# A gated delta-rule scan and its routing on one core: decay inside the first product, tanh for sigmoid, a second buffer at the end

## The reference

```
a = sigmoid(h @ Wa + ba);  b = sigmoid(h @ Wb + bb)
Sk = S k_t
S  = a*S - a*b * outer(Sk, k_t) + b * outer(v_t, k_t)      # S is 8 x 8
o_t = q_t^T S
```

## Time and profile before

| what | value |
|---|---|
| timed runs | 1351.15, 1360.18, 1360.09 us; median 1360.09 |
| profiled execution | 1352.62 us, span 1350.9 us |
| TensorE busy | 989.0 us (73%) in 5924 instructions |
| VectorE busy | 846.5 us (63%) in 2008 |
| ScalarE busy | 623.9 us (46%) in 1485 |
| GpSimd busy | 442.6 us (33%) in 636 |
| chain that ended last | PE 46%, DVE 19%, issue 13%, ACT 11%, POOL 8%, DMA 2% |
| scan of the four groups | 74 to 427 us |
| barrier between the layers | 531 us |

### The profile page before, as it was taken

The page is one execution under the profiler, slowest core; times in us unless marked ns, Lnnn a source line. Parts: engine busy times, 40 slices in busy tenths (PEclk is TensorE's granted clock), DMA queues, the critical chain, the costliest instruction groups (busy, mean ns, idle before and its releaser), DMA issues.

```text
span 1350.9 us, 18007 instructions
## 1 busy us (share of the span) xinstructions
PE 989.0 (73%) x5924; PEld 600.3 (44%) x5924; DVE 846.5 (63%) x2008; ACT 623.9 (46%) x1485; POOL 442.6 (33%) x636
## 2 busy tenths in 40 slices
PE   5563074985886896888788888878788878775682
PEld 3231032443453454333334555544556545544582
DVE  1386978858988332675666566766566666624452
ACT  3435253464444253154444456643556534663272
POOL 0201352634633323022442331363241444422413
PEclk9776595996997998787888899987999988998796
DMA  7000000000000001000000323212134003331372
GB/s 221 1 0 1 0 0 1 1 1 35 1 1 1 1 0 36 1 1 1 1 1 1 114 71 105 75 36 92 33 111 122 29 18 120 106 107 46 125 218 80
DMA packets 53885, 64.67 MB, mean 48 GB/s; under 512 B 6544, under 2 KB 38304, under 8 KB 53792
## 3 DMA queue, kind: packets, MB, share of 16 engines
q1 hardware_dynamic: 51744, 59.33, 14.6%
q0 software_dynamic: 2048, 4.20, 1.0%
HBM read 52.83 MB, written 10.68 MB: 47 GB/s over the span
## 4 chain that ended last, share of the span: by engine, by line
PE 46%; DVE 19%; issue 13%; ACT 11%; POOL 8%; DMA 2%; SPq 0%; DVEq 0%; POOLq 0%; ACTq 0%
PE banks L701 8%; PE banks L844 4%; PE banks L758 4%; DVE MX L1323 3%; PE banks L554 3%; PE banks L776 3%; POOL oms L1796 3%; PE banks L748 2%; PE banks L818 2%; PE banks L711 2%; PE banks L714 2%; PE banks L606 2%; POOL QX L1695 2%; PE banks L723 2%; ACT PT L1620 1%
## 5 line engine op out<-in xcount | busy, mean ns | idle before, releaser
L1323 DVE TENSOR_REDUCE MX<-banks 128x4 f32<-128x512 f32 (+2 forms) x192 | 199.3, 1044 | 87.2 <-PE banks L818 86.5
L1774 POOL TENSOR_SCALAR_AFFINE_SELECT PT<-PT 128x256 f32<-128x256 f32 x256 | 107.0, 432 | 419.4 <-ACT PT L1620 419.1
L1620 ACT ACTIVATE PT<-banks 128x768 f32<-128x768 f32 (+1 forms) x192 | 167.9, 876 | 92.6 <-PE banks L776 91.5
L701 PE MATMUL banks<-xgT,wg 128*128 128x128 f32 x736 | 106.3, 290 | 36.1 <-ACT ysb L1581 29.5
L701 PEld LDWEIGHTS banks<-xgT,wg 128*128 128x128 f32 x736 | 92.5, 198 | 57.7 <-issue 53.0
L844 PE MATMUL banks<-PT,VA 128*17 128x512 f32 (+3 forms) x1024 | 98.4, 482 | 13.6 <-DVE on L1346 13.6
L783 PE MATMUL banks<-KS,QS 32*128 32x512 f32 (+3 forms) x512 | 96.7, 421 | 14.7 <-DVE MX L1323 12.3
L776 PE MATMUL banks<-QS,KS 32*128 32x128 f32 (+3 forms) x512 | 91.7, 407 | 15.0 <-ACT PT L1620 9.6
L748 PE MATMUL banks<-w,hid 128*128 128x128 f32 x512 | 76.1, 296 | 30.6 <-DVE hid L1268 28.5
L748 PEld LDWEIGHTS banks<-w,hid 128*128 128x128 f32 x512 | 69.6, 206 | 63.3 <-DVE hid L1268 43.9
L1272 DVE SCALAR_TENSOR_TENSOR sil<-sil,yh 128x256 f32<-128x256 f32 x124 | 53.4, 431 | 62.7 <-ACT sil L1567 62.4
(11 more groups left out here) (256 smaller groups left out, 2120.8 us busy)
## 6 DMA issues: line engine op xcount, KB each, us to landing
wg<-in_ffn_dram SPq DMA_DIRECT2D x92, 386.0 KB, 3.4
xg<-xs SPq DMA_DIRECT2D x20, 256.0 KB, 3.1
yb<-ysb SPq DMA_DIRECT2D x20, 256.0 KB, 3.9
w<-in_ffn_w_dram SPq DMA_DIRECT2D x12, 256.0 KB, 5.0
xs<-zt SPq DMA_DIRECT2D x1, 1472.0 KB, 11.1
x<-in_L_attn_x_dram SPq DMA_DIRECT2D x4, 256.0 KB, 5.0
out_dram<-x SPq DMA_DIRECT2D x16, 64.0 KB, 1.5
wmod<-in_L_wmod_dram SPq DMA_DIRECT2D x2, 384.0 KB, 4.1
```

Source lines behind the costliest of these rows:

```text
L701: mm = e.matmul(ps[:, at:at + cols], w, h, start=True, stop=True)
L1323: v_mx.at(e.tensor_reduce(MX[n % 2][:, u:u + nm, qb % 2, 2 * pair:2 * pair + 2, 24].rearrange("p s i -> p i s"), p4, AX.X, ALU.max, negate ...
L1620: a_p.at(e.activation(PT[q % 3][:, 2 * pair:2 * pair + 2, :], where["score", q, pair][:, :, 0:n], ACT.Exp, scale=ISQ8))
L1774: ins = e.affine_select(out=pt, in_=pt, compare_op=ALU.is_ge, fill=0.0, base=0, pattern=[[0, 2], [1, 128]], channel_multiplier=-1)
```

## The change

1. *Decay as a fifth row.* A chunk of XU is now 56 words wide, and ScalarE writes the chunk's decay eight times behind its four rows (`gm`, once a group). The first product of a step has 5 rows instead of 4, so its fifth is the decayed state, 160 products instead of 128. All products of a step lie in one buffer TS of 76 words a state row: 36 that the first reduction takes (four rows of nine), then the fifth row of 8, then four rows of 8 for W times KT, now written token by token with KT read across (a step of four words). The last reduction takes the five rows of 8 across (a step of eight words). ScalarE's L1518 and its signal are gone. TS has three copies, and `values` runs two steps ahead.
2. *Sigmoids by tanh.* sigmoid(z) = 0.5 + 0.5 tanh(z/2), for the gates a and b (one multiply-add in place of add and reciprocal), and for the two expert weights, from the difference of the two maxima; the Exp of the routing goes, and its tanh comes after the second maximum.
3. *Group 3's products.* The second half of the products of queries with states goes to the space of Z[0], which is free by then. GQ waits for its decays and queries, not for the last state; in group 3 it stands 10 earlier in the table. The times of group 3's output are set closer, and the delays of ab, route and o_x on VectorE are 6, 2 and 2 instead of 1.
4. otok and xt share the space of OL, so `o_ol` waits for the group before to have updated x.

```diff
@@ table
-    DVE=dict(mod=1.0, gate=1.0, ab=1.0, up=5.0, route=1.0, o_x=1.0),
+    DVE=dict(mod=1.0, gate=1.0, ab=6.0, up=5.0, route=2.0, o_x=2.0),
...
-        gq, state, pw, dk, ol, sums, out, step = 0, (1, 6), 1, 6.5, 7, (6, 12, 15), 17, 1.3
+        gq, state, pw, dk, ol, sums, out, step = -10, (0, 5), 0, 5.5, 6, (5.5, 10.5, 13.5), 15, 1.3
@@ buffers
+        XUf = [sb(f"XU{i}", [128, 32 * 56 + 4], where=st) for i in range(2)]
+        XUc = [t[:, 0:32 * 56].rearrange("p (c x) -> p c x", x=56) for t in XUf]
+        XUb = [t[:, :, 0:48].rearrange("p c (j x) -> p c j x", x=12) for t in XUc]
...
+        TS = [sb(f"TS{i}", [128, 4, 76], where=st) for i in range(3)]
+        T0 = [t[:, :, 0:45].rearrange("p r (j e) -> p r j e", e=9)[:, :, :, 0:8] for t in TS]
+        T1 = [t[:, :, 0:36].rearrange("p r (j e) -> p r j e", e=9) for t in TS]
+        T2 = [t[:, :, 44:76].rearrange("p r (j e) -> p r j e", e=8) for t in TS]
+        T3 = [t[:, :, 36:76].rearrange("p r (j e) -> p r e j", e=8) for t in TS]
@@ VectorE, route, parts 2, 4 and 5
+                    v_rd.at(e.tensor_tensor(gd[:, :], gm[:, 2, :], gm[:, 0, :], ALU.subtract))
...
+                    v_gk.at(e.tensor_scalar(gk[r % 2][:, 0, :], gd[:, :], -0.5, 0.5, ALU.mult, ALU.add))
+                    v_gk.at(e.tensor_scalar(gk[r % 2][:, 1, :], gd[:, :], 0.5, 0.5, ALU.mult, ALU.add))
...
-                    n = v_own.at(e.reciprocal(gm[:, 1, :], gm[:, 0, :]))
+                    n = v_own.at(e.tensor_tensor(X, go[:, :, :, 0:E], gk[r % 2][:, :, :].unsqueeze(3)
+                                                 .broadcast_to([128, 2, 4, E]), ALU.mult))
...
+                    v_gt.at(e.tensor_tensor(gt, X[:, 0, :, :], X[:, 1, :, :], ALU.add))
@@ VectorE, share
-                n = v_own.at(e.tensor_scalar(abf, abf, 1.0, None, ALU.add))
-                v.wait_ge(v_own, n)
-                v_dec.at(e.reciprocal(abf, abf))
+                v_dec.at(e.tensor_scalar(abf, abf, 0.5, 0.5, ALU.mult, ALU.add))
@@ VectorE, scan
-                n = v_own.at(e.tensor_tensor(T1[k1][:, :, :, 0:8], S_[:, c, :, :].unsqueeze(2).broadcast_to([128, 4, 4, 8]),
-                                             XU[:, c, :, 0:8].unsqueeze(1).broadcast_to([128, 4, 4, 8]), ALU.mult))
+                n = v_own.at(e.tensor_tensor(T0[k1], S_[:, c, :, :].unsqueeze(2).broadcast_to([128, 4, 5, 8]),
+                                             U5.unsqueeze(1).broadcast_to([128, 4, 5, 8]), ALU.mult))
...
-                n = v_own.at(e.tensor_tensor(t2[:, :, :, 0:4], W_[:, c, :, :].unsqueeze(2).broadcast_to([128, 4, 8, 4]),
-                                             KT[:, c, :, :].unsqueeze(1).broadcast_to([128, 4, 8, 4]), ALU.mult))
+                n = v_own.at(e.tensor_tensor(T2[k1], W_[:, c, :, :].unsqueeze(3).broadcast_to([128, 4, 4, 8]),
+                                             KT[:, c, :, :].rearrange("p e j -> p j e").unsqueeze(1)
+                                             .broadcast_to([128, 4, 4, 8]), ALU.mult))
                 v.wait_ge(v_own, n)
-                v.wait_ge(a_ts, j + 1)
...
-                v_s.at(e.tensor_reduce(Sn, t2[:, :, :, :], AX.X, ALU.add))
+                v_s.at(e.tensor_reduce(Sn, T3[k1], AX.X, ALU.add))
@@ ScalarE
-                a_dx.at(e.activation(ab[:, g, :, :], ab[:, g, :, :], ACT.Exp, scale=-1.0))
+                a_dx.at(e.activation(ab[:, g, :, :], ab[:, g, :, :], ACT.Tanh, scale=0.5))
...
+            def gm_(g):
+                a.wait_ge(v_gm, g + 1)
+                a.wait_ge(v_s, 32 * (g - 1))
+                a_gx.at(e.activation(XUc[g % 2][:, :, 48:56], GMb[g % 2][:, :, 3:4].broadcast_to([128, 32, 8]), ACT.Copy))
...
-                a_ts.at(e.activation(T2[c % 2][:, :, :, 4], Sb[g % 2][:, c, :, :], ACT.Copy, scale=GMb[g % 2][:, c, 3:4]))
-                if c + 3 < 32:
-                    values(j + 3)
+                if c + 2 < 32:
+                    values(j + 2)
@@ GpSimd
-                g_.wait_ge(v_s, 32 * g + 32)
+                g_.wait_ge(v_gm, g + 1)
...
+                QX4 = QXs[g == 3 and eh].rearrange("p (c j) r e -> p c j r e", j=4)
```

More of the change, by code:

```diff
@@ L274, in build @@
         gq = sb("gq", [128, 4, 16])
-        gq2 = sb("gq2", [128, 4, 16])
+        gd = sb("gd", [128, 4])
+        gk = [sb(f"gk{i}", [128, 2, 4]) for i in range(2)]
         go = sb("go", [128, 2, 4, 16])
@@ L365, in build @@
         gX = sb("gX", [128, 2, 4, 16])
-        gk = [sb(f"gk{i}", [128, 2, 4]) for i in range(2)]
         gc = sb("gc", [128, 16, 4])
@@ L1241, in o_ol @@
                 v.wait_ge(p_ol, g)
+                v.wait_ge(v_x1, g)
                 v_ol.at(e.tensor_tensor(
```

89 lines of the change are left out of this document (36 added, 53 removed).

## The result

The kernel after takes 1358.9 us (median of 20 runs, 1350.3 to 1364.3), the kernel before beside it 1352.1 (median of 20, 1348.0 to 1361.2). The ratio is 1.0035, with a 95% interval of 1.0018 to 1.0052: 2.4 to 7.0 us slower. Forecast were 1330 us and a range of 1308 to 1352.

The account below looks back on a forecast made before the run. It took VectorE to lead layer 0's scan, held by waits for ScalarE's decayed state, and TensorE to bound layer 1. Terms -28 + 15.5 - 3.0 - 1.3 - 1 - 5 - 3 = -25.8 us from 1356.0 gave 1330 us, range 1308 to 1352.

Parts of the forecast that it names:

- Last reduction: End of each scan step on VectorE, read at a step of eight words: taken as 0, ends 0 and +110 ns.
- the edge between faster and same: Whole time: under 1346.5 us counted as faster by over 1%, chance 0.77; within 1%, chance 0.17.
- Second product: W times KT in each scan step on VectorE, KT read across: +88 ns, to 380 ns with GpSimd idle.
- First product: Start of each scan step on VectorE, 160 elements instead of 128: +33 ns, to about 320 ns.
- Waits for the decayed state: VectorE's 38.1 us of waits for ScalarE in layer 0's scan: 28 us go, ends 14 and 38.
- ab: VectorE's 6.7 us in two waits in the scan: the later slot saves 5 us (0 to 6.7).
- GQ early: GpSimd's 1.27 us product, now before the last state: its gain in groups 0 to 2 counted within the 28 us.
- Tail: End of layer 0 after the scan: net gain 3 us, ends a gain of 8 and a loss of 2.
- its end of a loss of 2: After the scan: GpSimd's eight products in one piece might slow VectorE's two-input instructions beside them, a loss of 2 us.
- Reciprocals, routing, tables: Sigmoids by tanh: -3.0 us for three reciprocals in the scan, -1 for routing, -1.3 for a prologue table load.
- rival 2: Scan step: crossed operands at the trace's worst excess make a step 364 ns dearer, 1361 us; chance 0.10.
- Rival 1: Scan: waits move to values, next preparation or VectorE's gatings, half the waits go, 1348 us; chance 0.20 together with rival 4.

Follow-up runs that it names:

- e1: VectorE alone, none of the kernel's work: reductions, products and multiplies timed at different steps between words; the 160-word reduction in the kernel's own pattern took 435 ns.
- e11: As e9, but with the delay of ab taken back from 6 to 1; 1345.9 us, ratio to the kernel before 0.9938.
- e14: Kernel after with step products in pairs of words, decays prepared in a scan three steps later and ab 11 us late; 1342.1 us, ratio to before 0.9921.
- e17: As e16, with group 3's norm, input products and gates 22 us later in the table; 1336.2 us, ratio to the kernel before 0.9845.
- e9: Kernel after with step products in pairs of words, last group's output as before (one buffer, late GQ, old times); 1346.7 us, ratio to before 0.9945.
- e16: Kernel after with step products in pairs of words and early GQ, but one buffer QX and the last group's old times; 1342.5 us, ratio to before 0.9895.
- e7: Kernel before with the sigmoids by tanh alone; 1354.5 us, ratio to the kernel before 0.9948.
- e12: Kernel after with the last group's output as before (one buffer, late GQ, old times); 1362.8 us, ratio to the kernel before 1.0066.
- e8: Kernel before with only the second buffer, early GQ and closer times of the last group's output; 1365.2 us, ratio to the kernel before 1.0026.

## Why the prediction was wrong

- *Last reduction*: this is the step that failed. The prediction bounded it at 0 and +110 ns and took 0, "since the reduction has one input and writes one word in five". It measured +119 ns, 15.2 us. The support was L1125, one input at a step of four words, 32 elements, no excess. e1 shows why that row misled. The prediction made its 186 ns out of the 162 of eight elements and 1.0 ns for each of the other 24; but in a row a one-input multiply takes 171 ns for 8 and 181 for 32, 0.4 ns an element, and at a step of four words it pays 0.4 ns more (244 to 301 for 160). The two-input slope hid a price, and one that is smaller than a reduction's. The reduction's own nearest row was L1220's 0.69 ns, the two-input price. With it the sum was -11.7 instead of -25.8, that is 1344 us: inside the range, and near the edge between faster and same. So it is the largest error, and not the whole. Forecast and result (4.7 us slower by the ratio) are 30 us apart: 15.2 are this reduction, 5.1 the second product, 5 ab, 4 the tail.
- *Second product*: 380 ns undisturbed, as read from L1220 (measured 0.38; 377 in e1). The mean grew by 128 and not 88 ns, 5.1 us more. The rest is GpSimd's: its excess over the undisturbed time is 107 ns before and about 150 after. VectorE stands less and its product is longer, so more of it is likely to fall beside GpSimd's; no run separates that. It was not in the sum.
- *First product*: +33 ns forecast, 0.33 us measured; its mean grew by 17.
- *Waits for the decayed state*: right. Without ab and AB, VectorE stood 41.3 us before and 14.2 after: 27 us, forecast 28.
- *ab*: wrong. 5 us forecast, and 6.7 us became 6.9 for AB. The prediction saw that ab is needed only by the next preparation, and did not ask what holds it: the chain that also makes AB. e11, e14 and e17 show it.
- *GQ early*: in the 28 by the prediction; some 2 us of its own between first state and barrier (e9 448.0, e16 446.2).
- *Tail*: wrong in sign within the tail, +1.0 us for -3. I had TensorE's wait grow by 1.9 us, which is about the place of the gating behind the third `o_pw` (2.25 us). It grew by 4.2. 1.38 us more are that `o_pw` and its sums beside GpSimd's second four products, which is what the prediction named at its end of a loss of 2. The other 0.91 are the second `o_pw`, which began just behind a product of GpSimd and not just ahead of it; e9 has that without the second buffer. Behind the wait TensorE's granted clock was 0.63, before 0.70.
- *Reciprocals, routing, tables*: in the sum as large as forecast (e7: 7 us for 5), but not from the places priced. In the scan the three reciprocals did save 2.9 us of VectorE; its routing took 14.0 us for 12.6 (12.7 in e7), where 1 less was forecast. e7's stretch is 2.5 us shorter for a forecast of 4; the rest lies in the prologue or in layer 1, which I took at 0. Four table loads are left, as said. The one on the prologue's chain is gone, yet the first state ends 0.9 us later (76.44 for 75.57); the first states of the runs here end between 72.6 and 77.4 us, so one execution can't show 1.3 us there.
- *Rivals*: the result is rival 2's side at a smaller size. A step cost 0.24 us more undisturbed and 0.26 with GpSimd's share, where rival 2 had 0.36. (292 - 96 x 1.04 is 192 and not 190, so its 1.15 ns were 1.09 and its 1361 us 1359.) Rival 1's place, the gatings, has 8.6 us of new waits. The Trainium skill (Vector Engine (DVE) Microarchitecture Reference, "5.2 Measured stream behaviour on trn2") had both answers for the last reduction: by its 1.73 ns for a source that hops every element 160 elements come to 430 ns, an estimate from the page's figure and the row's 320, and the trace agrees (439). Its remark on a one-source operation with few writes is not what this reduction shows. Nor does its rule that a port keeps its full rate only over pairs of adjacent words hold for e1's step of two words, at which 160 elements took 0.32 us as in a row.

By the profile the terms close up to the barrier: scan +6.9, tail +1.0, start +0.9 make it 8.8 us late. The timed runs give 2.4 to 7.0 us in all, so some 2 to 6 us seem to come back after the barrier, where the routing lost its reciprocals. The 18 profiles point the same way, weakly. A straight line through length of layer 1 and granted clock puts the 15 profiles with the new routing 4 us under the three with the old, with a standard error of 2. No run here tests it alone, and for the 20 runs of the kernel before beside the kernel after the clock isn't known.

## What to carry to other kernels

- Where an operand is read or written across, price every such instruction from the nearest row of the same kind (a reduction from a product, not from a small copy), and weigh it by how often it runs: 119 ns were 15 us. Then look for a layout in pairs of words, which keeps the reordering and here cost only 17 ns in the first reduction (320 for 303).
- A long wait of an in-order engine belongs to the chain that ends it. Before moving the waiting instruction, look at what stands next in line for the same chain; the cure was on TensorE's list.
- Freeing an engine of waits can put more of its work beside its neighbour's; allow for that when a wait is booked as gain (here 40 ns a product, 5 us).

## What the runs showed of the hardware

- VectorE reads and writes at a step of two words at full rate (0.32 us for a reduction of 160, 0.29 for a product of 128, as in a row); three words cost the reduction 0.04 us, four to sixteen 0.10 to 0.12. Two sources at a step of four cost no more than one (0.38 us for 128).
- A two-input instruction of VectorE and a product of GpSimd lengthen each other by who begins first. VectorE's 384 elements took 0.83 us where they began 0.01 us ahead of GpSimd's product, which then took 1.80 instead of 1.11 (before, e12). They took 1.73 to 1.74 where they began 0.1 us behind one (after, e8, e9). The reductions, with one input, keep their 439 and 303 ns in the mean.
- Layer 1, the same but for its routing, took 812 to 832 us in 18 profiled executions; its granted clock (0.88 to 0.86) went with it. A difference of under 1% is not to be read from the spans of two profiles.
